# Two queues for one load: edge targets split 64 and 61 partitions between SyncE and ScalarE

## The reference

```python
deg_out = clip(segment_sum(ones, src), 1); deg_in = clip(segment_sum(ones, dst), 1)
norm = rsqrt(deg_out[src] * deg_in[dst])
msg = (x[src] @ W1 + x[src] * x[dst] @ W2) * norm[:, None]
conv = x @ W1 + segment_sum(msg, dst)
...
h = maximum(layernorm(x), 0)
out = x + conv2(relu(conv1(h)))
```

## Time and profile before

| | us |
|---|---|
| median of 3 runs | 479.75 (479.25 to 479.88) |
| profiled execution, own time | 477.81 |
| profiled execution, span of its instructions | 475.9 |
| busy PE, DVE, ACT, POOL | 461.0, 415.5, 301.1, 152.8 |

### The profile page before, as it was taken

One profiled execution on the slowest core, in us unless ns is written; L12 is line 12 of the kernel. 1 busy time (PEld: TensorE's weight loads), 2 busy tenths in 40 slices (PEclk: granted clock), 3 DMA queues, 4 the chain that ended last, 5 costly groups with the idle time before them and its releaser, 6 DMA issues.

```text
span 475.9 us, 20140 instructions
## 1 busy us (share of the span) xinstructions
PE 461.0 (97%) x8079; PEld 432.6 (91%) x8079; DVE 415.5 (87%) x1127; ACT 301.1 (63%) x799; POOL 152.8 (32%) x381
## 2 busy tenths in 40 slices
PE   5889999999999998999999999999999999999996
PEld 5778888888788888999999999999999999999996
DVE  6999999999999988889898998987888788888773
ACT  1399999999999994435453544434465555555551
POOL 3532524241627500444444455543111111111110
PEclk9999999999999999999999999999999999999999
DMA  3329513131303000001111111110011111111124
GB/s 73 92 51 151 95 26 82 26 78 20 83 4 68 1 3 8 3 14 26 28 27 26 26 23 26 26 26 8 9 26 24 29 26 25 24 26 25 31 55 100
DMA packets 50104, 18.07 MB, mean 38 GB/s; under 512 B 46336, under 2 KB 48688, under 8 KB 50013
## 3 DMA queue, kind: packets, MB, share of 16 engines
q1 hardware_dynamic: 48623, 14.63, 16.1%
q0 software_dynamic: 672, 2.01, 1.5%
q10 hardware_dynamic: 718, 0.16, 0.2%
HBM read 6.28 MB, written 4.19 MB: 22 GB/s over the span
## 4 chain that ended last, share of the span: by engine, by line
PE 77%; DVE 16%; issue 3%; DMA 2%; ACT 1%; DVEq 0%; ACTq 0%
PE diff L1192 34%; PE iota_bank L1192 18%; PE slab L1093 13%; DVE los L785 10%; PE diff L1075 5%; PE diff L1143 2%; DVE stats L794 1%; DMA prev_i<-in_dst_dram 1%; PE diff L1044 1%; PE diff L1156 1%; DMA work<-mixed 1%; ACT hots L1243 1%; PE diff L1189 1%; PE slab L1192 1%; PE iota_bank L1156 1%
## 5 line engine op out<-in xcount | busy, mean ns | idle before, releaser
L785 DVE TENSOR_TENSOR los<-mixed,iota_bank 128x5120 bf16<-128x5120 bf16 x49 | 136.9, 2807 | 1.0 <-PE slab L1093 0.9
L1093 PEld LDWEIGHTS slab<-hots,los 128*128 128x128 bf16 x2352 | 115.4, 97 | 14.3 <-ACT words L1251 1.2
L1093 PE MATMUL slab<-hots,los 128*128 128x98 fp8e5 x2352 | 121.2, 208 | 0.5 <-DVE los L785 0.4
L1243 ACT ACTIVATE hots<-diff 128x784 f16<-128x784 f32 x147 | 118.8, 853 | 4.4 <-PE diff L1075 4.4
L1192 PE MATMUL diff<-late,mixed 128*128 128x128 f16 x1567 | 95.2, 219 | 0.0
L659 POOL TENSOR_TENSOR work<-work,h 128x64 f32<-128x64 f32 x97 | 31.3, 323 | 193.5 <-DVE work L929 193.5
L1192 PE MATMUL diff<-los,mixed 128*128 128x129 f16 x1470 | 90.1, 220 | 0.0
L1192 PEld LDWEIGHTS diff<-late,mixed 128*128 128x128 fp8e4 x1567 | 89.6, 98 | 0.1
L1192 PEld LDWEIGHTS diff<-los,mixed 128*128 128x128 fp8e4 x1470 | 84.8, 98 | 0.0
L1075 PE MATMUL diff<-select,mixed 80*128 80x392 f16 x294 | 65.3, 329 | 2.3 <-ACT hots L1243 2.3
L837 DVE TENSOR_SCALAR mixed<-words 128x400 int32<-128x400 int32 x192 | 66.2, 373 | 0.0
(11 more groups left out here) (213 smaller groups left out, 563.1 us busy)
## 6 DMA issues: line engine op xcount, KB each, us to landing
x_sb<-in_x_dram SPq DMA_DIRECT2D x4, 384.0 KB
rows_table<-rows SPq DMA_DIRECT2D x6, 252.0 KB, 2.6
mixed<-rows_table SPq DMA_DIRECT2D x18, 84.0 KB, 3.0
work<-mixed SPq DMA_TRANSPOSE x82, 2.3
out_dram<-x_sb SPq DMA_DIRECT2D x8, 128.0 KB
los<-in_dst_dram SPq DMA_DIRECT2D x1, 750.0 KB
p_table<-p_rows_sb SPq DMA_DIRECT2D x24, 28.0 KB
p_table<-p_rows_sb SPq DMA_DIRECT2D x24, 7.0 KB
```

What stands on the lines that cost most here:

```text
L785: nc.vector.tensor_tensor(out=los[:, b % LOS_RING].rearrange("e s (v t) -> e s v t", t=2), in0=key, in1=val, op=ALU.is_equal).then_inc(los ...
L1093: ins = nc.tensor.matmul(to, los[:, u // 2 % LOS_RING, u % 2 * ULOWS + low], pairs, start=(step == 0), stop=(step == USTEPS - 1), skip_gro ...
L1243: nc.scalar.activation(bass.AP(to.tensor, to.offset, [to.ap[0], [step, 2], [STEPS * HPITCH, 8], [1, BLOCKS]]), diff[m % 2][:, :, 0:HALF].r ...
```

## The change

SP's two loads of `dst_i` become one of the partitions 0 to 63. ACT issues the other 61 partitions, 64 to 124, and then the load of `prev_i`. Each of the two still adds 16 to `dst_in`, and all waits are as they were.

```diff
-            sp.dma_start(dst_i[0:120], dst_main[0:120]).then_inc(dst_in, 16)
-            sp.dma_start(dst_i[120:SROWS], dst_main[120:SROWS]).then_inc(dst_in, 16)
+            sp.dma_start(dst_i[0:64], dst_main[0:64]).then_inc(dst_in, 16)
             sp.wait_ge(dst_in, 32)
...
+            act.dma_start(dst_i[64:SROWS], dst_main[64:SROWS]).then_inc(dst_in, 16)
             act.dma_start(prev_i[1:SROWS], bass.AP(dst.tensor, dst.offset + ROWLEN - GRAIN,
                                                    [[ROWLEN, SROWS - 1], [1, GRAIN]])).then_inc(prev_in, 16)
             act.wait_ge(dve_steps, 1)
```

## The result

| | before | changed |
|---|---|---|
| median of 5 runs | 479.75 us (479.25 to 479.88) | 492.28 us (492.17 to 492.91) |
| profiled execution: own time, span | 477.81, 475.9 | 492.24, 490.4 |

The changed kernel is slower by 12.5 us: ratio 1.0263, 95% interval 1.0251 to 1.0275. The forecast was 493.8 us with a range of 490.5 to 502.7.

A forecast was written before the change was run, and what follows sets the result against it. PE bounds the whole run, but its start waits for the loads: landing 13.0 us later plus 1.0 for the clock is 14.0, taking the profiled 477.81 to 491.8; with 1.94 for the median, 493.8 us, range 490.5 to 502.7.

The forecast's parts named there:

- The bound and the missing slack: Start of the kernel: everything waits for the loads, and a later landing moves the end by the same amount.
- 61 rows on one DMA engine: ACT's new load: rows spread over the largest divisor up to 16; 61 is prime, so one engine carries all.
- 0.25 us per row, the peak rate and not the average in company: Lone engine's load: a 6400-byte row costs 0.25 us, the peak rate; 65 rows take 16.25 us.
- The second rival: Load of the targets: a lone engine runs at the company's average, 0.30 to 0.42 us per row, 502.6 us; chance 0.22.
- the first: Load of the targets: the 61 rows are spread over the engines like the others, 479.4 us; chance 0.04.
- The third: PE's start: the clock, low for longer, slows the 92 fillers too, 4.0 us more, 497.8 us; chance 0.05.
- Landing 13.0 us later: Start of DVE: the targets reach their reader at 20.0 us instead of 7.00.
- 1.0 us for the clock: PE after its long idle time: low clock slows L1054's products and the 36 fillers; cost between 0.75 and 1.3 us.
- the sign: PE's timeline: low clock from about 11 us on, L1054 twice as long, L1075 first at about 34.7.
- Own time and median: Whole run: the median stands 1.94 us above the profiled execution, so 491.8 becomes 493.8 us.

The follow-up runs named there:

- e3: The changed kernel with the cut at 96: SP loads 96 partitions, ACT the other 29; 484.22 us, ratio 1.0102 to the kernel before.
- e5: The changed kernel with 250 fillers instead of 35 ahead of L1053, so that PE works nearly until the landing; 493.3 us, ratio 1.0283 to the kernel before.
- e10: The changed kernel with its cut at partition 112: SP loads 112 partitions, ACT 13, then `prev_i`; 476.80 us, ratio 0.9991 to the kernel before.
- e12: The kernel before, unchanged, run again for a second trace; ratio 1.0005 to the kernel before.
- e2: The changed kernel with ACT's 61 partitions loaded as 60 and 1; 479.06 us against 479.52 of the kernel before on this chip, ratio 0.9987.
- e7: The kernel before with its two loads on SP cut at 112 instead of 120 (112 and 13 rows); 478.99 us, ratio 0.9988.
- e8: The changed kernel with other cuts: SP loads partitions 0 to 63 and 112 to 124, ACT 64 to 111, then `prev_i`; ratio 1.0008 to the kernel before.
- e1: The changed kernel with both loads (64 and 61 partitions) issued by SP, ACT only `prev_i`; 492.43 us, ratio 1.0274 to the kernel before.
- e6: The changed kernel with ACT's two loads swapped, `prev_i` ahead of the 61 partitions; 492.07 us, ratio 1.0265 to the kernel before.
- e9: The changed kernel with 250 fillers instead of 35 ahead of L1053 and 72 instead of 36 behind it; ratio 1.0265 to the kernel before.

## Why the prediction was right, and where it was not

- **The bound and the missing slack.** Right. The chain behind the landing shifted as a block, and no slack of several microseconds turned up. `last` is read 12.9 us later than in either trace of before, the medians differ by 12.5; whether the 0.4 us between is slack or spread, these traces can't tell.
- **61 rows on one DMA engine.** Right: 190 packets on ACT's queue, one engine's share from 4 to 19 us, and the loss gone with 60 and 1.
- **0.25 us per row, the peak rate and not the average in company.** Right: 26 GB/s, 0.246 us on the plateau, 0.255 by the difference of e3. The second rival (0.386) is out; the first (spread like the others, 479.4) is out as well, because not all engines take part. That two queues share their engines held, though: SP's last four rows had to take turns with ACT's. The third (the clock holds the 92 fillers too) didn't happen in the changed kernel, where they took 5.30 us; in e5 they took 6.92, behind a gap of 2.27 us after which those of e10 took 5.30.
- **Landing 13.0 us later.** 12.96 by DVE's start in the first pair of traces. That the peak rate and not the average holds for a lone engine was argued, not measured, when the forecast was made; 0.386 us per row would have given 502.6.
- **1.0 us for the clock.** This is the term that was mis-sized. The prediction doubled the twelve of L1054 from 1.64 to 3.28 us; they took 2.57. So L731 lost next to nothing (25.08, right behind L847), and only the turn came late, 0.4 us behind its operands (28.68 against 28.28). In sum the trace shows 0.6 against the first trace of before, and nothing against e12: the first product comes 12.92 us later than there, `last` 12.91. The slow products are not the change's alone either. e2, e7, e8 and e12 read `last` by 7.65 us and have them too (2.56 or 2.57 us), and from `last` to the first product they need 13.5 to 13.9 us, just as the changed kernel, e1 and e6 do. Nor did the sign appear: in every stretch of the changed kernel from 7 to 28 us the granted clock reads 1.00, and that PE was slow shows in the durations alone. Two readings of before were a little off as well: a mean clock of 0.60 from 10.5 to 11.0 us puts its fall at about 10.6 and not 10.8, and the 0.101 us taken for a filler at the low clock is a mean with the last ones at the full clock; where all 36 are slow it is 0.112 (4.04 / 36). Of the 1.5 us by which the forecast was too high this term is 1.0; without it 13.0 stand against the measured 12.5. Single traces can't resolve the rest: by the first product of changed, e1 and e6 against that of the two traces of before, the shift is 12.3 to 13.6 us.
- **Own time and median.** The 1.94 us that I added for the changed kernel's median belonged to the trace of before alone: in the changed kernel the profiled execution (492.24) and the median (492.28) agree. Between these two traces lie 1.4 us of main loop too: from the first L1093 to the last 156.7 us in the trace of before, 158.1 in that of the changed kernel (there L1092). It isn't the change, it goes with the chip: in e9 to e12, on chips where the kernel before takes 477.5 us, the loop is 156.6 or 156.7 us long; in e1 to e8, on chips where it takes 479.5 and 479.8, it is 158.1 to 158.8, but for e5 with 157.1, whatever the loads. The first trace of before, with 477.81 us below all five timed runs, looks like one of the first group; the record doesn't name its chip.

## What to carry to other kernels

In these runs a load from SP or ACT was spread over the largest number up to 16 that divides its rows (124 on 4, 120 on 15, 64 on 16, 63 on 9, 62 on 2, 61 on 1, 13 on 13), and the reader waited for the engine that had the most rows, to within about 1 us. Before a transfer is cut, factor the pieces: 61 rows cost 12.5 us where 60 and 1 cost nothing. A profile of the load shows the number: packets minus rows. A mean rate over several microseconds can hide two levels, so look at it microsecond by microsecond before it is explained. And one trace is one draw: PE's slow stretches in it are not to be charged to a change until a second trace of the same kernel has them at the same place.

## What the runs showed of the hardware that was not expected

- One DMA engine alone moved 26 GB/s in rows of 6400 bytes, microsecond after microsecond, 25.7 being its share in the best stretch of fifteen; two engines of one load moved 51 or 52 GB/s in some microseconds and 26 to 46 in others of the same load.
- One engine with rows of both queues served them side by side: four of SP's and four of ACT's from 6 to 8 us, at 26 GB/s together.
- The granted clock of the profile and the speed of the matmuls did not agree. PE's stretch of e12 (start and end, length, busy, clock, DMA share, GB/s) reads 1.00 where the twelve of L1054 take 2.56 us instead of the 1.42 of e5, e9 and e10, and the fillers 0.112 us each (4.04 / 36). In e5, the second block, the column falls where the 92 fillers are slow:

```profile
9.50:12.00 2.50, 2.43 (x13) 1.00 0.06 13
```

```profile
28.00:29.00 1.00, 0.88 (x10) 0.63 0.00 0
29.00:30.00 1.00, 1.00 (x13) 0.50 0.49 143
```

  The duration of the fillers, 0.107 us each in the chain of the changed kernel (3.84 / 36) against 0.056 (5.14 / 92) at the full clock, is the surer sign.
